# AdaLN feed-forward on one core: a second buffer for the quantised intermediate, and the preparation of the down weights spread over four slots

## What is computed

```python
def reference(x, length, ...):
    u = x * (arange(512) < length)                   # x is 64 x 32 x 512
    y = irfft(rfft(u) * rfft(K))[..., :512] + u * D   # causal convolution, K per head
    y = y * mask
    xq = int4_quant(y)                                # row scale from mean |y|
    gate, up = xq @ Wg.T, xq @ Wu.T                   # 512 -> 1376, ternary weights
    inter = int8_quant(up * square(relu(gate)))       # row scale from max |.|
    return x + inter @ Wd.T                           # 1376 -> 512, ternary weights

def bitlinear(x, w, scale):
    w_mean = mean(abs(w))
    w_q = clip(round(w / (w_mean + EPS)), -1, 1)
    return einsum('...i,oi->...o', x, w_q * w_mean * scale)
```

## Time and profile before

| | |
|---|---|
| median of 3 runs | 201.41 us (201.2 to 201.56) |
| the profiled execution, its own time | 201.68 us |
| its span in the profile | 199.9 us |
| TensorE busy | 170.8 us (85%), 1062 matmuls |
| VectorE busy | 156.1 us (78%) |
| ScalarE busy | 116.6 us (58%) |
| GpSimd busy | 27.4 us (14%) |
| chain that ended last | PE 62%, DVE 17%, DMA 9%, issue 5%, ACT 5% |
| HBM read, written | 21.07 MB, 4.28 MB |

### The profile page before, as it was taken

One profiled execution on the slowest core, in us unless ns is written; L12 is line 12 of the kernel. 1 busy time (PEld: TensorE's weight loads), 2 busy tenths in 40 slices (PEclk: granted clock), 3 DMA queues, 4 the chain that ended last, 5 costly groups with the idle time before them and its releaser, 6 DMA issues.

```text
span 199.9 us, 3333 instructions
## 1 busy us (share of the span) xinstructions
PE 170.8 (85%) x1062; PEld 90.8 (45%) x1077; DVE 156.1 (78%) x411; ACT 116.6 (58%) x195; POOL 27.4 (14%) x71
## 2 busy tenths in 40 slices
PE   1002897999999679999999999999999999999992
PEld 1002865555554334545454545454545444444461
DVE  6998997466598988986898978787878798887951
ACT  2466987366999596863548282828272736334520
POOL 5023998970000000000000000000000000000000
PEclk9999999999999999999999999999999999999999
DMA  4999495999879989999646465545452524435244
GB/s 120 383 369 329 115 271 189 202 313 389 187 169 210 242 179 232 189 241 181 150 132 130 132 137 147 118 146 115 146 116 43 110 48 103 93 87 117 60 108 105
DMA packets 48913, 34.25 MB, mean 171 GB/s; under 512 B 37024, under 2 KB 37312, under 8 KB 48896
## 3 DMA queue, kind: packets, MB, share of 16 engines
q1 hardware_dynamic: 45008, 25.91, 57.0%
q10 hardware_dynamic: 3888, 8.13, 12.9%
HBM read 21.07 MB, written 4.28 MB: 127 GB/s over the span
## 4 chain that ended last, share of the span: by engine, by line
PE 62%; DVE 17%; DMA 9%; issue 5%; ACT 5%; DVEq 0%; ACTq 0%
PE down_ps L662 13%; PE gate_ps L624 13%; PE up_ps L629 12%; PE tr_dve_ps L551 6%; PE conv_ps L551 6%; PE conv_ps L662 5%; DMA it_int<-inter_q 5%; DMA raw<-in_L_ffn_w_down_dram 4%; PE tr_act_ps L537 2%; DVE int L1045 2%; ACT g L798 2%; DVE inter L1150 2%; PE gate_ps L675 1%; DVE y L1073 1%; PE down_ps L551 1%
## 5 line engine op out<-in xcount | busy, mean ns | idle before, releaser
L798 ACT ACTIVATE g<-gate_ps,gu_scale 128x416 f32<-128x416 f32 (+2 forms) x48 | 30.4, 634 | 43.5 <-PE gate_ps L624 43.5
L1150 DVE SCALAR_TENSOR_TENSOR inter<-up_ps,gu_scale,g 128x416 f32<-128x416 f32 (+2 forms) x48 | 33.3, 693 | 22.3 <-ACT g L801 22.0
L629 PE MATMUL up_ps<-up_t,q_t 128*128 128x512 bf16 (+2 forms) x190 | 44.6, 357 | 2.2 <-DVE inter L1150 2.1
L624 PE MATMUL gate_ps<-gate_t,q_t 128*128 128x416 bf16 (+2 forms) x180 | 42.6, 356 | 0.6
L801 ACT ACTIVATE g<-g 128x416 f32<-128x416 f32 (+2 forms) x48 | 28.1, 586 | 1.5
L1158 DVE TENSOR_REDUCE imax<-inter 128x1 f32<-128x928 f32 (+1 forms) x32 | 27.8, 870 | 1.1
L629 PEld LDWEIGHTS up_ps<-up_t,q_t 128*128 128x128 bf16 x192 | 18.5, 98 | 21.3 <-DVE inter L1150 3.4
L662 PE MATMUL down_ps<-down_t,i_t 128*128 128x512 bf16 (+1 forms) x121 | 27.9, 379 | 0.0
L624 PEld LDWEIGHTS gate_ps<-gate_t,q_t 128*128 128x128 bf16 x192 | 17.5, 98 | 15.7 <-issue 2.2
L725 ACT ACTIVATE int<-raw 128x2048 bf16<-128x2048 f32 (+3 forms) x8 | 15.6, 1945 | 8.8 <-DMA raw<-in_L_ffn_w_gate_dram 5.2
L551 PE MATMUL conv_ps<-toep,x_t 128*64 128x512 f32 (+3 forms) x128 | 19.0, 439 | 1.5 <-ACT x_t L753 1.0
(11 more groups left out here) (187 smaller groups left out, 200.6 us busy)
## 6 DMA issues: line engine op xcount, KB each, us to landing
toep<-k_back SPq DMA_DIRECT2D x16, 512.0 KB, 5.1
out_dram<-o_sb SPq DMA_DIRECT2D x30, 128.0 KB, 2.4
raw<-in_x_dram ACTq DMA_DIRECT2D x3, 512.0 KB, 5.8
raw<-in_x_dram SPq DMA_DIRECT2D x3, 512.0 KB, 8.7
raw<-in_L_ffn_w_down_dram ACTq DMA_DIRECT2D x1, 1472.0 KB, 12.4
raw<-in_L_ffn_w_down_dram ACTq DMA_DIRECT2D x1, 1280.0 KB, 9.0
raw<-in_L_ffn_w_gate_dram ACTq DMA_DIRECT2D x1, 1024.0 KB, 5.8
raw<-in_L_ffn_w_gate_dram SPq DMA_DIRECT2D x1, 1024.0 KB, 10.5
```

Of the source, the lines that this page charges most:

```text
L624: mm = pe.matmul(gate_ps[bank][:, 0:cn], q_t[m % 3][:, i, :], gate_t[:, i, c0:c0 + cn], start=(i == 0), stop=(i == KB - 1))
L629: mm = pe.matmul(up_ps[bank][:, 0:cn], q_t[m % 3][:, i, :], up_t[:, i, c0:c0 + cn], start=(i == 0), stop=(i == KB - 1))
L798: nc.scalar.activation(g2[bank][:, 0:cn], gate_ps[bank][:, 0:cn], ACT.Relu, scale=gu_scale[m % 4][:, 0:1]).then_inc(relu_done, 1)
L1150: v.scalar_tensor_tensor(out=inter[:, c0:c0 + cn], in0=up_ps[bank][:, 0:cn], scalar=gu_scale[m % 4][:, 1:2], in1=g2[bank][:, 0:cn], op0=AL ...
```

## The change

There are four edits.

1. `inter_q` becomes two buffers, used in turn. The quantisation in slot m now waits for the turn of tile m-2. One more small memset clears the second buffer's pad.
2. The roundings: DVE and ACT make one each in slot 2 (k = 0 and 2) and one each in slot 3 (k = 1 and 3). Each is issued at the place where two stood before, in its own slot.
3. The turns and copies come a slot later: SP turns k = 0 and 2 in slot 3 and k = 1 and 3 in slot 4. DVE copies k = 0 in slot 4 and k = 1 in slot 5, behind the second `gated`. ACT copies k = 2 at the end of slot 4, and k = 3 in slot 5 between `relu_square(0)` and `y_sum`.
4. The third quad of x is asked in slot 2 rather than 1, the fourth in slot 6 rather than 4, by both SP and ACT.

```diff
-        inter_q = sb("inter_q", [P, IB * P], I16)
+        inter_q = [sb(f"inter_q{p}", [P, IB * P], I16) for p in range(2)]
...
-                    sp.dma_start_transpose(it_int[(m - 1) % IRING], inter_q[:]
+                    sp.dma_start_transpose(it_int[(m - 1) % IRING], inter_q[(m - 1) % 2][:]
...
-                if m in (2, 3):
-                    turn_down(2 * m - 4)
-                    turn_down(2 * m - 3)
-                if m in (1, 4):
-                    load_half(sp, 3 if m == 1 else 4, 0)
+                if m in (3, 4):
+                    turn_down(m - 3)
+                    turn_down(m - 1)
+                if m in (2, 6):
+                    load_half(sp, 3 if m == 2 else 4, 0)
...
                 elif m < T - 2:
+                    if m == 5:
+                        down_copy(3)
                     y_sum(m + 2)
                 relu_square(1)
...
-                if m in (3, 4):
-                    down_copy(2 * m - 5)
+                if m == 4:
+                    down_copy(2)
...
-                if m == 4:
+                if m == 6:
                     for i in range(2):
                         act.wait_ge(w_rounded[2][i], rounds(2, i))
                     load_half(act, 4, 1)
...
-                if m == 1:
+                if m == 2:
                     load_half(act, 3, 1)
-                if m == 2:
-                    down_round(2)
-                    down_round(3)
+                if m in (2, 3):
+                    down_round(m)
...
-            v.memset(inter_q[:, I:IB * P], 0)
+            for p in range(2):
+                v.memset(inter_q[p][:, I:IB * P], 0)
...
-                if m in (3, 4):
-                    down_copy(2 * m - 6)
+                if m in (4, 5):
+                    down_copy(m - 4)
...
-                    down_round(0)
-                    down_round(1)
+                if m in (2, 3):
+                    down_round(m - 2)
...
-                if m >= 1:
-                    dve.wait_ge(it_loaded[(m - 1) % IRING], 16 * ((m - 1) // IRING + 1))
+                if m >= 2:
+                    dve.wait_ge(it_loaded[(m - 2) % IRING], 16 * ((m - 2) // IRING + 1))
...
-                    v.tensor_scalar(inter_q[:, 0:I], inter[:], iscale[:], None, ALU.mult).then_inc(inter_quant, 1)
+                    v.tensor_scalar(inter_q[m % 2][:, 0:I], inter[:], iscale[:], None, ALU.mult).then_inc(inter_quant, 1)
```

More of the change, by code:

```diff
@@ L636, in turn_last @@
                     mm = pe.transpose(tr_act_ps[:, c * P // 2:(c + 1) * P // 2].bitcast(BF16),
-                                      inter_q[:, c * P:(c + 1) * P].bitcast(BF16), ident_bf[:])
+                                      inter_q[(T - 1) % 2][:, c * P:(c + 1) * P].bitcast(BF16), ident_bf[:])
                 mm.then_inc(it_turned, 1)
@@ L643, in turn_last @@
                     mm = pe.transpose(tr_dve_ps[0:r, o:o + P // 2].bitcast(BF16),
-                                      inter_q[:, c * P:c * P + r].bitcast(BF16), ident_bf[:])
+                                      inter_q[(T - 1) % 2][:, c * P:c * P + r].bitcast(BF16), ident_bf[:])
                 mm.then_inc(it_turned, 1)
@@ L847, in _ @@
             act.wait_ge(iscale_ready, 1)
-            nc.scalar.activation(inter_q[:, IT_SPLIT * P:I], inter[:, IT_SPLIT * P:I], ACT.Copy,
+            nc.scalar.activation(inter_q[(T - 1) % 2][:, IT_SPLIT * P:I], inter[:, IT_SPLIT * P:I], ACT.Copy,
                                  scale=iscale[:]).then_inc(last_quant, 1)
@@ L1203, in _ @@
                     dve.wait_ge(iscale_ready, 1)
-                    v.tensor_scalar(inter_q[:, 0:IT_SPLIT * P], inter[:, 0:IT_SPLIT * P], iscale[:], None,
+                    v.tensor_scalar(inter_q[m % 2][:, 0:IT_SPLIT * P], inter[:, 0:IT_SPLIT * P], iscale[:], None,
                                     ALU.mult).then_inc(inter_quant, 1)
```

## The result

The changed kernel takes 210.1 us (median of 4 runs, 209.41 to 211.43) against 201.31 us before: a ratio of 1.0444, 95% interval 1.0391 to 1.0497, so 4.4% slower. The profiled execution took 209.41 us with a span of 207.6; the span before was 199.9.

A forecast was written before the change was run, and what follows sets the result against it. TensorE was taken as the bound, alone from slot 7. A later `down(0)`, 6.29, less 0.62 given back, plus 1.7 for the clock, is +7.4 us on 201.68: 209.1, median 0.27 lower, 208.8 us; range 205.5 to 211.0.

The forecast's parts named there:

- The moment that counts: TensorE's start of `down(0)`, 87.90 us before; behind it only slot 5's conv and slots that TensorE fills, 9.87 us from slot 7.
- Roundings and second buffer: Slot 2 on VectorE: one rounding less, 0.89 us, and no wait of 0.28; chain 1.17 us earlier by end of slot 4.
- The turn and the hold: SP's turn of k = 3, issued with its pair from 81.59, lands at 88.14; ScalarE's copy in slot 5 waits 4.6 us.
- The chain from landing to TensorE: ScalarE's copy 1.36, to second `gated` 1.99, to VectorE's copy 1.82, that copy 0.88: 6.05 us; `down(0)` at 94.19, 6.29 later.
- The clock: After TensorE's 7.5 us idle before `down(0)`, matmuls run slow as in the preamble: 1.7 us lost, bounds 0 and 3.5.
- The choice between the clock's row and the matmuls' lengths: Preamble: granted-clock row reads 1.00, no loss (rival 207.1 us, chance 0.14); matmuls at about half speed, taken, give 1.7 us.
- The x loads: Asked in slots 2 and 6, nobody waits for them; they can slow only slot 3's first pair of turns, hidden by the stall.
- The one in which ScalarE is not held: Turn of k = 3 lands by 83.54, VectorE's copy of k = 1 ends at 90.07: +1.55, 203.0 us, chance 0.06.
- The faster one: All copies done when TensorE comes to `down(0)` at 86.73: wins 1.17 and 0.62, 199.6 us, chance 0.04.

The follow-up runs named there:

- two variants whose SP queue is that of the change: The change with 32 unused matmuls ahead of the first down (ratio 1.0353); the change with VectorE's copy of k = 1 ahead of tile 6's y copy (1.0137).
- The run with TensorE kept busy: The change with 32 matmuls of 512 columns, product unused, ahead of the first down on TensorE: 1.0353 of the kernel before, median 209.29 us.
- the spread: Later roundings, turns and copies of the down weights (edits 2 and 3); alone on the kernel before: ratio 1.0564.
- the copy was moved: The change with ScalarE's copy of k = 3 put behind the rounding of y in slot 5: 206.19 us, 1.0211 of the kernel before.
- the version with early turns and the copy first: The change, turns of k = 3 and 1 ahead of SP's slot-4 `turn_q`, VectorE's copy of k = 1 before tile 6's y copy: 0.9937, again 0.9933 of before.
- early turns: The change with turns of k = 3 and 1 ahead of `turn_q` in SP's slot 4, VectorE's k = 1 copy before y's scale: 0.9887, again 0.9975 of before.

## Why the prediction was right

- **The moment that counts.** The prediction chose the start of `down(0)` and said that slots behind it keep their length. They do: 101.02, 110.89, 120.76.
- **Roundings and second buffer.** A gain of 1.17 us by slot 4 was forecast; the wait in slot 3 shrank by 1.09 us, and the pair of turns in slot 4 was issued at 81.62, forecast 81.59.
- **The turn and the hold.** Landing forecast at 88.14, and ScalarE's copy began at 88.06; held 4.6 forecast, 4.49 measured. That it came out within 0.1 us is partly luck: in two variants whose SP queue is that of the change, the same turn took 6.3 and 6.0 us and held ScalarE for 5.8 and 5.6. By the rule of the Trainium skill that the prediction weighed (Advanced Engine Details and Errata, X-Bar Transpose (TRN2)), that transposing DMAs are as fast as regular ones, a turn would have taken about 3.5 us, an estimate (the prediction's 3.6 counts 360 KB, and in the profile's unit of 1024 bytes the turn is 352). The pair's turns took 5.0 and 5.2, so the trace does not agree.
- **The chain from landing to TensorE.** 6.05 forecast from the rows of slots 4 and 5, 94.11 - 88.06 = 6.05 measured. `down(0)` at 94.19 forecast, 94.11 measured.
- **The clock.** The mechanism was right and this term too small: 1.7 forecast from the preamble, 2.13 measured in the profile. That an idle of 7.5 us would do what the far longer one of the preamble did was assumed; no row of before showed it. The run with TensorE kept busy puts 2.1 us on it. The choice between the clock's row and the matmuls' lengths was right: the row of the preamble had read 1.00, but here the row itself shows 0.50. The four runs of the change have mean clocks from 0.975 to 0.984, and those with the lowest are not all the slowest; the median lies 0.7 us above the profiled run, where the prediction had set it 0.27 below; why it is higher stays open. The clock's 0.4 us and the median's 1.0 are the difference between 208.8 and 210.1, but for 0.1.
- **The x loads.** That asking them later costs nothing fits the runs: alone they change nothing that the runs can tell. With the old loads the spread cost more, ScalarE being held 6.3 us; whether the later loads spare the change that is not shown, as turns of over 6 us came without an x load too.
- **The rivals.** The one in which ScalarE is not held came out with its mechanism when the copy was moved: the first `down` waits for VectorE's copy of k = 1. Its price, +1.55 us, was too low, since the clock falls there too (+4.38 to slot 7). The faster one needs its copies in time, and the version with early turns and the copy first has just that: 1.61 and 1.71 us of its 1.79.

## What to carry to other kernels

Work that is moved into an engine's idle time brings its own wait with it: before an instruction is put into a gap of an in-order queue, look up when its input can land, and what stands behind it. A one-time step that TensorE needs should end before TensorE arrives, and TensorE here runs ahead of the engine that makes it; that VectorE has time in the same slot says nothing. And once TensorE is the bound, a stall in front of it can be paid twice, by its length and by the clock behind it: 7.20 us of idle here, and 2.13 more for the matmuls after it.

## What the runs showed of the hardware

TensorE's clock can fall after idles that are short. After 1.24 and 0.97 us close together in slot 3 the granted clock went to 0.55, and the conv took 4.07 us instead of 2.37; it happened again after 1.40 and 0.97 us. In other executions with much the same idles it didn't: before, after 1.64 and 0.97 us, that conv took 2.37. So a kernel with such idles has two lengths in that slot, 1.7 us apart. Of the six profiles in which the first of these idles was 1.24 to 1.64 us, two show the fall; of the eight with the spread and two buffers, where it was 0.44 to 0.55 us, none does.

The mean granted clocks of the timed executions say more. The two profiles with that fall have a mean of 0.988, that of before 1.000. Of the executions behind the ratios of the later runs, 42 of 75 of the kernel before have a mean of 0.992 or less, and 15 of 35 with two buffers and no spread; with early turns, in both versions and both timings, it is none of 43. So this form of the spread does keep the clock up, and part of its timed gain can be that. That it does so by the shorter idle in slot 3 is likely but not shown, as an execution without a profile doesn't say where its clock fell.

The down weights' turns, 128 x 1408 int16 and always issued two in a row, landed in anything from 3.9 to 7.0 us in these runs, where the turns of the intermediate, of the same shape, had a median of 3.5 before. The 7.0 stood beside a load of x, but 6.3 and 6.4 came without one.
